# Last network of a decoder: some element-wise passes on GpSimd, rounding of the up factor ahead of the products, and a diagonal product for the maximum over partitions

## What is computed

```python
def act_qdq(x):                       # qmax = 32767
    scale = jnp.maximum(jnp.max(jnp.abs(x)) / qmax, 1e-12)
    return jnp.clip(jnp.round(x / scale), -qmax - 1.0, qmax) * scale
x = act_qdq(x)
up = act_qdq(x @ lpbq_dequant(w_up).T)          # 256 -> 768
gate = act_qdq(x @ lpbq_dequant(w_gate).T)      # 256 -> 768
sig = fixed_qdq_u16(jax.nn.sigmoid(gate))       # round to 1/65536, clip
gate = act_qdq(gate * sig)
o = act_qdq(gate * up)
return o @ lpbq_dequant(w_down).T               # 768 -> 256
```

## Time and profile before

| | us |
|---|---|
| median of 3 runs | 2116.99 |
| the profiled execution's own time | 2121.81 |
| its span | 2119.80 |
| last network, from the last layer norm before it | about 1906 to 2119.8 |
| scale 1 known | 1964.55 |
| scale 2 known | 2022.21 |
| first product of gate and up starts | 2033.48 |
| last maximum of gate times up ends | 2065.70 |

### The profile page before, as it was taken

How to read it: one execution, slowest core, us unless ns; L and a number is a source line. 1 busy time by engine, 2 the same in 40 slices (tenths; PEclk the granted TensorE clock), 3 DMA queues, 4 the chain that set the end, 5 groups by cost and what they waited for, 6 DMA issues and landing times.

```text
span 2119.8 us, 34752 instructions
## 1 busy us (share of the span) xinstructions
PE 1768.9 (83%) x12793; PEld 1267.9 (60%) x12793; DVE 1453.3 (69%) x4876; ACT 1042.1 (49%) x2594; POOL 485.9 (23%) x554
## 2 busy tenths in 40 slices
PE   3667778887868868999999999999879999989708
PEld 1345656666653445666666766666658998974307
DVE  6887888887324786767766577777546676653795
ACT  5535555454426633555554355555225555433852
POOL 4101111010110122333333333333203323320002
PEclk8768988888978978999999999999999999999959
DMA  5000000000000101000000000000414334400001
GB/s 158 1 1 1 1 1 1 1 1 1 1 1 1 40 20 65 1 1 1 2 1 1 1 1 1 1 1 1 132 30 91 80 72 91 91 2 0 0 0 40
DMA packets 86363, 49.83 MB, mean 24 GB/s; under 512 B 40253, under 2 KB 83953, under 8 KB 86001
## 3 DMA queue, kind: packets, MB, share of 16 engines
q1 hardware_dynamic: 80337, 47.31, 8.7%
q10 hardware_dynamic: 5856, 0.29, 0.2%
HBM read 45.50 MB, written 2.10 MB: 22 GB/s over the span
## 4 chain that ended last, share of the span: by engine, by line
PE 55%; DVE 31%; ACT 7%; issue 4%; POOL 2%; POOLq 0%; DVEq 0%; ACTq 0%
DVE sq L739 8%; DVE nx L736 8%; PE PS L1618 6%; PE PS L1645 6%; PE PS L1916 6%; PE PS L1632 5%; PE PS L1603 3%; PE PS L1593 3%; PE PS L2329 3%; PE PS L1979 2%; PE PS L1660 2%; PE PS L1935 2%; DVE nnm L1117 2%; PE PS L1585 2%; PE PS L1944 2%
## 5 line engine op out<-in xcount | busy, mean ns | idle before, releaser
L1772 POOL TENSOR_SCALAR px<-px,crl 128x128 f32<-128x128 f32 (+7 forms) x128 | 226.2, 1767 | 419.2 <-DVE crl L1744 419.2
L1683 ACT ACTIVATE px<-PS,cnm 128x128 f32<-128x128 f32 (+7 forms) x256 | 189.3, 740 | 265.4 <-DVE cnm L1729 258.5
L739 DVE TENSOR_SCALAR sq<-nx 128x4 f32<-128x4 f32 x1024 | 188.1, 184 | 35.0
L736 DVE TENSOR_TENSOR_SCAN nx<-sq 128x6 f32<-128x6 f32 x1024 | 182.9, 179 | 35.1 <-POOL sq L866 0.9
L1726 DVE TENSOR_REDUCE cm<-PS 128x1 f32<-128x128 f32 (+6 forms) x224 | 154.1, 688 | 56.3 <-PE PS L1618 55.7
L1632 PE MATMUL PS<-ident,px 128*128 128x128 f32 x1152 | 157.8, 277 | 13.2 <-ACT qT L1671 9.5
L1632 PEld LDWEIGHTS PS<-ident,px 128*128 128x128 f32 x1152 | 129.1, 141 | 60.3 <-issue 34.9
L1645 PEld LDWEIGHTS PS<-pT,V 128*64 128x64 f32 x2304 | 124.1, 137 | 63.5 <-issue 34.5
L1618 PE MATMUL PS<-kT,qT 64*128 64x512 f32 (+3 forms) x768 | 158.3, 517 | 4.5 <-ACT px L1683 2.6
L1645 PE MATMUL PS<-pT,V 128*64 128x128 f32 x2304 | 154.1, 278 | 6.4 <-DVE pT L1737 2.8
L196 POOL TENSOR_SCALAR rstd<-mv 128x1 f32<-128x1 f32 x80 | 30.7, 384 | 557.7 <-DVE mv L174 557.7
(11 more groups left out here) (335 smaller groups left out, 3942.2 us busy)
## 6 DMA issues: line engine op xcount, KB each, us to landing
xbs<-in_fside_Bx16xSxS SPq DMA_DIRECT2D x8, 1232.0 KB, 6.7
fsrc<-in_fside_Bx16xSxS SPq DMA_DIRECT2D x8, 1232.0 KB, 6.7
xmk<-in_mask_Bx16xSxS_bk SPq DMA_DIRECT2D x8, 308.0 KB, 8.4
fsrc<-in_mask_Bx16xSxS_bk SPq DMA_DIRECT2D x8, 308.0 KB, 8.4
X<-in_x SPq DMA_DIRECT2D x4, 512.0 KB, 6.8
w<-in_L_attn_W_ffn SPq DMA_DIRECT2D x2, 1024.0 KB, 13.2
t<-in_L_ffn_w SPq DMA_DIRECT2D x2, 1024.0 KB, 11.7
out<-xs SPq DMA_DIRECT2D x16, 128.0 KB, 1.7
```

Of the source, the lines that this page charges most:

```text
L736: e.tensor_tensor_scan(k.nx[:, :], d0, d1, 0.0, ALU.mult, ALU.add).then_inc(sem("rec.scan"), 1)
L739: e.tensor_scalar(o, bass.AP(k.nx, 2, [[6, P], [0, 2], [3, 2]]), 10.0, -10.0, ALU.min, ALU.max).then_inc(sem("rec.clip"), 1)
L1683: e.activation(k.px[n % 2][:, h, 0:width], src, ACT.Exp, scale=-1.0, bias=k.cnm[:, n % 4, h:h + 1], accum_out=k.cl[:, n % 4, h:h + 1]).the ...
L1772: e.tensor_scalar(k.px[n % 2][:, 0, 0:width], k.px[n % 2][:, 0, 0:width], k.crl[:, n % 4, 0:1], None, ALU.mult).then_inc(sem("c.normal0"), 1)
```

## The change

Three edits, all in the last network.

1. One pass of each of the parts 0 to 5 (`pool_part`) goes to GpSimd: for the even parts 0, 2, 4 the subtraction of MAGIC (before ScalarE, L2365), for the odd parts 1, 3, 5 the clip and round of the sigmoid (before VectorE, L2281). Parts 6 and 7 stay as they were. The sigmoid becomes a step of its own; that of an even part below 6 now stands behind the copies of the up part v + 2.
2. The subtraction of MAGIC from U goes to GpSimd for all eight parts, and all eight `f.up` steps come before scale 3 and before the first `f.times`.
3. The maximum over partitions: VectorE multiplies the identity by the column (`k.dm`, 128 x 128), TensorE multiplies a matrix of ones by it, which puts all 128 values on every partition, and VectorE takes the maximum on all partitions. The transposition, the maximum on one partition and the spreading product are gone.

```diff
@@ swiglu_order
     for v in range(PARTS + 1):
         if v + 1 < PARTS:
             o.add(*project(1, v + 1))
+        if 0 < v < PARTS and (v - 1) % 2 == 0 and pool_part(v - 1):
+            o.add(("f.sigmoid", v - 1))
         if v < PARTS:
             o.add(("f.even", v))
+            if v % 2 or not pool_part(v):
+                o.add(("f.sigmoid", v))
         if v == PARTS - 1:
             o.add(("f.acc", 2), ("f.gm", 2))
         if v > 0:
             o.add(("f.gate", v - 1))
         if v == PARTS - 1:
             o.add(("f.step", 2))
-    ahead = 3
-    o.add(("f.acc", 3), ("f.gm", 3), *[("f.up", v) for v in range(ahead)], ("f.step", 3))
+    o.add(*[("f.up", v) for v in range(PARTS)], *scales(3))
     for v in range(PARTS):
-        if v + ahead < PARTS:
-            o.add(("f.up", v + ahead))
         o.add(("f.times", v))
@@ swiglu_vector
-    def gm(n):
-        w.wait_ge("f.whole", 3 * n + 1)
-        e.tensor_reduce(k.gm[0:1, n:n + 1], PS[0:1, 7, 0:P], AX.X, ALU.max).then_inc(sem("f.whole"), 1)
+        w.wait_ge("f.acc", n + 1)
+        e.tensor_scalar(k.dm[:, :], k.ident[:, :], k.acc[:, n:n + 1], None, ALU.mult).then_inc(sem("f.whole"), 1)
@@ step (VectorE)
+        w.wait_ge("f.whole", 3 * n + 2)
+        e.tensor_reduce(most, PS[:, 7, 0:P], AX.X, ALU.max).then_inc(sem("f.whole"), 1)
@@ gate (VectorE)
+        if v % 2 and pool_part(v):
+            w.wait_ge("f.pool", v + 1)
+        else:
+            w.wait_ge("f.sigmoid", v + 1)
+            e.tensor_scalar(sg, sg, 65535.0 / 65536.0, 192.0, ALU.min, ALU.add).then_inc(sem("f.value"), 1)
+            w.wait_ge("f.value", gated(v) - 1)
@@ swiglu_tensor
-        e.transpose(PS[0:1, 7, 0:P], k.acc[:, n:n + 1], k.ident[:, :]).then_inc(sem("f.whole"), 1)
-        e.matmul(PS[:, 7, P:P + 1], k.ones[0:1, :], k.gm[0:1, n:n + 1], start=True, stop=True).then_inc(sem("f.whole"), 1)
+        w.wait_ge("f.whole", 3 * n + 1)
+        e.matmul(PS[:, 7, 0:P], k.ones[:, :], k.dm[:, :], start=True, stop=True).then_inc(sem("f.whole"), 1)
@@ new
+def swiglu_pool(e, w, k):
+    sem = k.sem
+
+    def even(v):
+        if v % 2 == 0 and pool_part(v):
+            w.wait_ge("f.gq", evened(v) + 1)
+            e.tensor_scalar(part(k.G, v), part(k.G, v), MAGIC, None, ALU.subtract).then_inc(sem("f.pool"), 1)
+
+    def sigmoid(v):
+        sg = k.sg[:, v % 3, :, :]
+        if v % 2 and pool_part(v):
+            w.wait_ge("f.sigmoid", v + 1)
+            e.tensor_scalar(sg, sg, 65535.0 / 65536.0, 192.0, ALU.min, ALU.add).then_inc(sem("f.pool"), 1)
+
+    def up_(v):
+        w.wait_ge("f.tu", v + 1)
+        e.tensor_scalar(part(k.U, v), part(k.U, v), MAGIC, None, ALU.subtract).then_inc(sem("f.pool"), 1)
```

## The result

After, the median of 4 runs is 2135.82 us (2133.84 to 2137.72), beside 2118.01 for the kernel before in 4 runs on the same chip: a ratio of 1.0083, 95% interval 1.0069 to 1.0097. The forecast was 2115.1 us with a range up to 2119.5. The rival with a slow GpSimd, at 2133 us and a chance of 0.18, is what happened. The profiled execution took 2137.49 us, its span 2135.7.

What follows compares the result with a forecast made beforehand. VectorE and ScalarE were both taken as full up to scale 2, then VectorE alone. Savings of 1.2 and 0.8 less 0.1 for the maximum took 1.9 off the median 2116.99, giving 2115.1 us, range 2112.2 to 2119.5.

Steps and rivals of the forecast that it cites:

- The rival with a slow GpSimd: All moved passes: at 4.2 us each, +5 in the first stage and +11 from scale 2, about 2133 us; chance 0.18.
- The step that failed: Price of the new GpSimd passes on 1536 values: 1.5 us each, as L859 also has immediates only.
- the far end: Upper price kept for a new GpSimd pass: 4.2 us, scaled from the slow row of L1772.
- threshold of about 2.5 us a pass: GpSimd pass length from which the slow rival decides, as alternation with products eats the net gain.
- Collisions: GpSimd passes and VectorE products or clips exclude each other, maxima are free; one collision of 1.3 us counted before scale 2.
- both collide: Rival: both collisions before scale 2 happen and GpSimd's last U pass is late; 2117.2 us, no change; chance 0.24.
- the walk: Step-through of parts 0 to 5: part 2's pass and part 5's clip may meet products, costing VectorE 1.2 and 1.4 us.
- The saving in the parts' passes: Parts 0 to 5: VectorE loses three clips, ScalarE three passes; scale 2 comes 2.5 us earlier without collisions.
- U rounded ahead: After scale 2: first product at 14.2 us, periods of 3.45; net 1.6 us won, 0.8 after lateness.
- The lateness of the first pass: GpSimd's U passes start late behind gate 7's product and may hold the first product by up to 1.5; 0.8 us taken.
- The maximum over partitions: Chains of scales 0, 1 and 4: about 1.5 us where it was 1.43; +0.1 us in all, bounds -0.3 and +0.9.

Runs made afterwards that it cites:

- forms: Kernel before plus thirteen GpSimd passes of different operations on a scratch buffer during the gate products; ran once, 2116.46 us.
- forms_more: Kernel before plus eight GpSimd scratch passes of 128x1536 with other operation pairs during the gate products; ran once, 2121.67 us.
- fast_pass: Kernel after with every new GpSimd pass written as a min and max pair, so the numbers computed differ; 2112.21 us, 0.9974 of before.
- diagonal_only: Kernel before with only the new maximum over partitions, nothing moved to GpSimd and U as before; 2116.46 us, 0.9993 of before.
- u_tensor: Kernel before with the new maximum and U ahead on GpSimd, its subtraction as tensor minus spread column; 2121.07 us, 1.0004 of before.
- pairs: Kernel before plus paired VectorE instructions and GpSimd scratch passes after the gate's maxima, to see who waits; ran once, 2121.05 us.

## Why the prediction was wrong

**The step that failed** is the choice of a price: "All new passes have immediates only, as L859, so I take 1.5 and keep 4.2 as the far end." L859 and L1772 differ in three things, the kind of operand, the size and the operations; I took the first for the cause. forms and forms_more show that it is the third. A column costs 0.07 us; the operations make 1.47, 4.09 or 5.40. fast_pass, with nothing but the operations changed, is 23 us below the kernel after. The "same operation in the same form" of the rival's working was wrong too, as L859 has another pair of operations. The far end of 4.2 held for the subtractions (4.12), and not for the clip, at 5.40: a bound from the nearest slow row, which has one operation, was not a bound for two.

**The slow rival** had the right mechanism in the second stretch and half of it in the first. It named about 2133 us, and the median came to 2135.8, which is luck: its two terms were off in opposite ways. In the first stretch it had +5 and 11.6 was measured: the clip at 5.40 wasn't in it, nor that GpSimd does the clip ahead of the next even part's subtraction, which puts both on one chain. In the second it had 54.7 us from scale 2 (+11) and 48.24 (+4.6) was measured: passes and products were to exclude each other wholly, 6.0 a part, but the product is let in a microsecond before the pass ends and the period is 4.68. Its threshold of about 2.5 us a pass, meant for the whole change, was too high for this stretch: against diagonal_only U on GpSimd wins 1.46 us with passes of 1.47 (fast_pass) and loses 2.57 with 2.75 (u_tensor); a straight line between them, an estimate, crosses at about 1.9. No run tried such a pass.

**Collisions** happen as the earlier trace rows had them, and maxima are free of them (pairs: 1.75 beside a pass). With quick passes two products were held for 1.26 each: the rival "both collide", which the walk had shown and I had halved. The walk was right for part 2; the second was part 4's subtraction and not part 5's clip.

**The saving in the parts' passes** was taken as 2.5 us without collisions. From the last copy of U part 1 on, fast_pass is 0.1 us faster in this stretch than diagonal_only and has lost 2.5 to its two collisions, which gives 2.6 before them. The step is right in size; what is wrong is the choice of one collision, and no kernel with GpSimd passes in this stretch gained there.

**U rounded ahead**: forecast 14.2 us from scale 2 known to the first product, and 14.20 in the kernel after (2047.69 - 2033.49, the reciprocal's end; 14.36 from its start); periods of 3.45 and 1.6 us net with quick passes, 1.46 measured (43.58 - 42.12). Right, but for the passes' price. The lateness of the first pass, for which I took 0.8, was not there at 1.47 us.

**The maximum over partitions**: the product pair took 0.80 us at the lower clock as forecast, and scale 4's chain got 0.1 longer (2081.73 to 2083.27, 1.54, where it was 1.43). Behind scale 1 I had 0.2 us for TensorE's earlier start, and the start is 0.41 us earlier in the kernel after (0.71 before the reciprocal in place of 0.30); the copies come 0.5 earlier there (6.33 in place of 6.85), and 0.9 in diagonal_only. What I missed is the granted clock, which is at its lower level for a few microseconds near this start. That the diagonal moves it is not shown. The rest is read from the traces and not tried by itself.

## What to carry to other kernels

A pass's price belongs to its operations: before a pass is moved to another engine, find a row with the same two operations there, and where none exists, take the slowest row of that engine per operation as a live case and not as the far end. Look at what stands behind the moved pass on its new engine: GpSimd was busy less than half of the stretch, and the chain through it still set the end. Where an engine is idle for half of a stretch and its passes keep their length beside the bound engine's, as ScalarE's 1.58 to 1.66 us here, give it the work, and count the passes per part on both so that neither waits.

## What was not expected of the hardware

- GpSimd's tensor-scalar pass on 128x1536 takes 4.09 us with one operation and 5.37 to 5.40 with most pairs, but 1.47 with min then max or mult then mult, as a copy (1.46). A subtraction of two tensors (3.43) or of a spread column (2.75) is quicker than that of an immediate.
- A small VectorE instruction can be held like a large one: the diagonal's pass on 128x128 took 2.02 us beside a slow pass and 0.29 otherwise, and a product of two columns 1.26 and 0.16. Tensor-scalar instructions on one column were not held: those at 2041.39 and 2041.63 took 0.21 and 0.15 us beside the same pass that held the product of two columns.
- A VectorE product behind a GpSimd subtraction of an immediate is let in 1.0 us before its end, a tensor-scalar pass 0.15 us before it; behind a subtraction of a spread column the product too waits to 0.14 us before the end. That a product needs only what the pass reads, and is free once the pass has read all, is a reading of this and was not tried by itself.
- In forms, with GpSimd's passes back to back, VectorE's four passes on XT, 3.0 us of work (0.75 each in forms_more), took 11.96 us from the first start to the last end.
- Around the end of TensorE's idle time for scale 1 (2.5 to 2.9 us) the granted clock is 0.50 for a while, and where that begins differs between kernels: 0.8 us ahead of the next products in diagonal_only, 1.1 us behind their start in fast_pass. Together with the diagonal's earlier start it makes the range of 5.9 to 8.1 us from scale 1 to the last copy of U part 1.
